# Moving two projections and a weight product in the second layer's slot order, and spreading the first layer's row sums with float32r products

## The reference, cut to what matters

```python
# layer 0, x: (16, 256, 256), 16 heads of 16
q, k = _rope(q, k)
scores = einsum('bhtd,bhsd->bhts', q, k) / sqrt(16)
probs = softmax(where(causal, scores, -inf), axis=-1)    # the division by the row sums
out = einsum('bhts,bhsd->bhtd', probs, v)                # heads side by side, (b, t, 256)
x = x + out @ w_out.T + b_out
...
# layer 1, 16 heads of 64, segments of 128 tokens
qkv = (s * rsqrt(mean(s * s) + eps) * g_norm) @ W_qkv    # q and k are rotated
...
x = x + concat_heads(attn @ v) @ W_out
```

## Time and profile before

| what | value |
|---|---|
| median of 3 runs | 2428.9 us (2425.71 to 2430.02) |
| the profiled execution's own time | 2429.98 us |
| its span, first to last instruction | 2428.1 us |
| busy over the span | PE 93%, DVE 76%, ACT 53%, POOL 42% |
| mean granted TensorE clock | 0.977 of full |
| chain that ended last, by engine | PE 57%, DVE 19%, POOL 10%, issue 8%, ACT 4% |

### The profile page before, as it was taken

The page is one execution under the profiler, slowest core; times in us unless marked ns, Lnnn a source line. Parts: engine busy times, 40 slices in busy tenths (PEclk is TensorE's granted clock), DMA queues, the critical chain, the costliest instruction groups (busy, mean ns, idle before and its releaser), DMA issues.

```text
span 2428.1 us, 53715 instructions
## 1 busy us (share of the span) xinstructions
PE 2250.7 (93%) x18240; PEld 2042.6 (84%) x18240; DVE 1853.8 (76%) x5119; ACT 1289.7 (53%) x3839; POOL 1019.6 (42%) x1078
## 2 busy tenths in 40 slices
PE   4799999999976799999999999899999999999999
PEld 3688878888865678878878878899999999999999
DVE  5878888888878667666666665578878888888876
ACT  1666666666662455555555655334336555555522
POOL 5535454454524465465465454033332222222073
PEclk8999999999987899999999999999999999999999
DMA  4523333233330322222222223221126677777443
GB/s 137 174 93 103 107 95 116 89 114 95 99 110 3 99 53 60 70 58 58 73 57 57 73 50 82 64 36 41 40 87 219 231 232 238 235 229 239 144 120 124
DMA packets 203301, 267.36 MB, mean 110 GB/s; under 512 B 61670, under 2 KB 171510, under 8 KB 192278
## 3 DMA queue, kind: packets, MB, share of 16 engines
q1 hardware_dynamic: 194166, 245.27, 33.3%
q0 software_dynamic: 8864, 18.66, 3.0%
HBM read 175.84 MB, written 43.94 MB: 91 GB/s over the span
## 4 chain that ended last, share of the span: by engine, by line
PE 57%; DVE 19%; POOL 10%; issue 8%; ACT 4%; DMA 1%; POOLq 0%; SPq 0%; DVEq 0%; ACTq 0%
PE bank L55 48%; PE bank L136 6%; POOL P L1796 3%; DVE Ph L821 2%; DVE xe L928 2%; POOL Qn L1821 1%; POOL Qn L1819 1%; DVE qm L917 1%; DVE xe L933 1%; PE bank L1322 1%; DVE sgs L955 1%; ACT Ph L657 1%; DVE rot0s L881 1%; PE bank L1362 1%; POOL Pm L1801 1%
## 5 line engine op out<-in xcount | busy, mean ns | idle before, releaser
L1495 ACT ACTIVATE P<-P,mx 128x144 f32<-128x144 f32 x512 | 206.2, 405 | 257.9 <-DVE mx L1616 256.9
L2642 POOL DMA_INDIRECT xE<-d_y,ixs x78 | 111.6, 1431 | 336.5 <-PE bank L136 306.0
L55 PE MATMUL bank<-xD_hi,w1e_lo 128*128 128x256 f32 x880 | 251.1, 285 | 0.0
L55 PE MATMUL bank<-w2e_hi,hrD_hi 128*128 128x256 f32 x880 | 249.0, 283 | 0.0
L55 PE MATMUL bank<-w2e_lo,hrD_hi 128*128 128x256 f32 x880 | 248.9, 283 | 0.0
L55 PE MATMUL bank<-w2e_hi,hrD_lo 128*128 128x256 f32 x880 | 248.9, 283 | 0.0
L55 PE MATMUL bank<-xD_lo,w1e_hi 128*128 128x256 f32 x880 | 245.9, 279 | 0.0
L55 PE MATMUL bank<-xD_hi,w1e_hi 128*128 128x256 f32 x880 | 245.6, 279 | 0.0
L1127 POOL TENSOR_TENSOR xe<-xe 128x704 f32<-128x704 f32 (+3 forms) x64 | 88.0, 1376 | 355.7 <-DVE xe L936 355.4
L1796 POOL TENSOR_TENSOR P<-P,rs 128x512 f32<-128x512 f32 x128 | 133.1, 1040 | 244.8 <-DVE rs L1625 241.2
L2251 ACT ACTIVATE hD<-bank,b1E 128x256 f32<-128x256 f32 x312 | 127.0, 473 | 197.2 <-PE bank L55 187.9
(11 more groups left out here) (324 smaller groups left out, 7871.9 us busy)
## 6 DMA issues: line engine op xcount, KB each, us to landing
w1raw<-in_ew SPq DMA_DIRECT2D x39, 1024.0 KB, 6.0
w2raw<-in_ew SPq DMA_DIRECT2D x39, 1024.0 KB, 4.8
stack<-d_rot SPq DMA_DIRECT2D x256, 96.0 KB, 2.7
K<-Kn SPq DMA_DIRECT2D x256, 72.0 KB, 2.0
d_rot<-QKh SPq DMA_DIRECT2D x64, 256.0 KB, 3.1
Q<-Qn SPq DMA_DIRECT2D x256, 64.0 KB, 2.0
d_ys<-oE SPq DMA_DIRECT2D x39, 256.0 KB, 2.6
d_rot<-QKl SPq DMA_DIRECT2D x32, 256.0 KB, 3.1
```

The lines of the kernel that those rows point to most:

```text
L55: inst = e.matmul(out, l, r, start=k == 0, stop=k == len(pairs) - 1)
L1495: inst = e.activation(P1[t % 2][:, n, :], P1[t % 2][:, n, :], ACT.Exp, bias=mx1[t % 2][:, 2 * g + sg:2 * g + sg + 1], scale=-1.0, accum_ou ...
L2642: e.indirect_dma_start(out=xE[q % 2][c], out_offset=None, in_=d_y, in_offset=bass.IndirectOffsetOnAxis(ap=ixs[r % 4][:, c:c + 1].bitcast(U ...
```

## The change

It has two parts that have nothing to do with each other. In the second layer's attention, `project(b+1, 2)` goes ahead of slot 1's `turn_heads`, `project(b+1, 3)` goes from slot 2 to the end of slot 1, and `back(b-1, 0)` goes ahead of slot 2's `turn_heads`. The waits of each step stay with it. In the first layer, DVE splits the reciprocals into a float32r part and the rest (two more DVE instructions of 32 columns, each waiting for the one before), in a zeroed 128 x 2 x 128 tile `rsp`; the transposes then give 128 rows, ACT copies 128 rows, and two float32r products on 128 rows with a 0/1 matrix that adds the two parts take the place of two float32 products on 16 rows. `sel0` grows to 128 rows, and once, at the start, ACT makes a float32r copy of it and POOL clears `rsp`.

```diff
-        w_out0, rsT, OT0 = tile("w_out0", 2, 256), tile("rsT", 256), tile("OT0", 2, 256)
+        w_out0, rsT, OT0 = tile("w_out0", 2, 256), tile("rsT", 256, dt=F32R), tile("OT0", 2, 256)
...
+        rsp, sel0r = tile("rsp", 2, 128, dt=F32R), tile("sel0r", 2, 128, dt=F32R)
...
-                turn(e, [(banks[6][0:16, st * 128:st * 128 + 128], rs0[b % 2][:, st, :]) for st in range(2)]
+                turn(e, [(banks[6][:, st * 128:st * 128 + 128], rsp[:, st, :].bitcast(F32)) for st in range(2)]
...
-                    inst = e.matmul(halves(7)[:, G, :], sel0[0:16, G, :], rsT[0:16, :], start=True, stop=True)
+                    inst = e.matmul(halves(7)[:, G, :], sel0r[:, G, :], rsT, start=True, stop=True)
...
-                e.activation(rsT[0:16, :], banks[6][0:16, 0:256], ACT.Copy).then_inc(c_rsT, 1)
+                e.activation(rsT, banks[6][:, 0:256], ACT.Copy).then_inc(c_rsT, 1)
...
+                e.activation(sel0r, sel0, ACT.Copy)
...
-                e.reciprocal(rs0[b % 2], rs0[b % 2]).then_inc(v_ri, 1)
+                if b:
+                    e.wait_ge(p_rsT, b)
+                else:
+                    e.wait_ge(g_V, 2)
+                inv, hi, lo = rs0[b % 2], rsp[:, :, 0:16], rsp[:, :, 16:32]
+                e.reciprocal(inv, inv).then_inc(*vs.up())
+                e.wait_ge(s_v, vs.n)
+                e.tensor_copy(hi, inv).then_inc(*vs.up())
+                e.wait_ge(s_v, vs.n)
+                e.tensor_tensor(lo, inv, hi.bitcast(F32), ALU.subtract).then_inc(v_ri, 1)
...
+            e.memset(rsp.bitcast(F32), 0.0)
...
+                    if s == 1:
+                        project(b + 1, 2)
                     if s == 2:
-                        project(b + 1, 3)
+                        back(b - 1, 0)
                     if s == 3:
                         squares(entering(b))
...
                     if s == 1:
-                        project(b + 1, 2)
-                    if s == 2:
-                        back(b - 1, 0)
+                        project(b + 1, 3)
```

More of the change, by code:

```diff
@@ L178, in program @@
         b_v0 = tile("b_v0", 2, 256)
-        tile("space_q", 552)
+        rsp, sel0r = tile("rsp", 2, 128, dt=F32R), tile("sel0r", 2, 128, dt=F32R)
+        tile("space_q", 40)
         qr = [tile(f"qr{i}", 44) for i in range(2)]
@@ L313, in sync_ab @@
             load_in(0)
-            for dst, src in ((raw0, "w_qkv0"), (b_qk0, "b_qk0"), (rot0, "rot0k"), (sel0[0:16], "sel0"),
+            for dst, src in ((raw0, "w_qkv0"), (b_qk0, "b_qk0"), (rot0, "rot0k"), (sel0, "sel0"),
                              (w_out0, "w_out0"), (b_out0, "b_out0")):
@@ L2744 @@
     A["w_out0"] = T2(np.ascontiguousarray(g["L0_attn_w_out"].T[rows]))
-    sel = np.zeros((16, 2, 128), np.float32)
+    sel = np.zeros((128, 2, 128), np.float32)
     for r in range(256):
-        sel[rows[r] // 16, r // 128, r % 128] = 1.0
+        sel[rows[r] // 16::16, r // 128, r % 128][0:2] = 1.0
     A["sel0"] = sel
```

## The result

The changed kernel takes 2443.8 us (median of 7 runs, 2437.0 to 2445.4), the kernel before 2430.0 in its 7 runs beside them. The ratio is 1.005, with 95% between 1.004 and 1.006: slower by half a per cent, about 14 us. The forecast was 2450 us, in a range from 2437 to 2464, so the sign and the range held and the size was about 6 us too large. The profiled execution took 2441.84 us (span 2439.9, clock 0.973), 11.9 us more than the profiled one of before.

What follows compares the result with a forecast made beforehand. The prediction took DVE's chain to bound the first layer's slots 0 and 1, PE mostly the rest. First layer +28 us (14 x 1.76 + 1 + 2), second -5.6, sum +22: 2450 us, range 2437 to 2464.

Steps and rivals of the forecast that it cites:

- The rival in which PE's 0.7 us come off whole: First layer: PE's work is the bound, so 14 x 0.7 us is saved beside the second layer's 5.6: 2413 us, chance 0.07.
- The first layer's price: First layer's DVE chain: maxima 3.45 us later, less 1.3 and 0.39 given back, net 1.76 us per batch, 14 batches.
- POOL's line 1129 gets in, and the subtraction ends at about 436.9: First layer's split: after the copy's wait, POOL's next instruction goes first and the subtraction waits it out; maxima 3.45 us later.
- the pair at 39 us: Earlier trace: DVE lines 933 and 936 each waited out a POOL instruction; taken as the nearest model for copy and subtraction.
- the rival with one POOL instruction waited out: First layer's split: only one POOL wait, maxima 1.85 us later, net 1.2 us per batch: 2441 us, chance 0.17.
- the forecast case: First layer's split: copy and subtraction each wait out a POOL instruction, 1.76 us per batch; the whole forecast's chance was 0.50.
- PE's wait at the transposes: First layer, `turn_sums`: PE waits for the subtraction, about 2.6 us idle per batch.
- The clock: First layer, slots 0 and 1: PE's waits lower the granted clock in one or two steady batches, +2 us, ends 0 and +20.
- The second layer: Second layer's attention: most of slot 1's wait moves to slot 2, 0.4 us less per batch, -5.6 us over 14 batches.
- The fourth rival: Second layer gives nothing, the delayed copies of slot 2 being the new wait: 2456 us, chance 0.12.
- The first projections of the second layer, and the last `back`, fall in stretches where PE waits for others: nothing: Second layer's start and end: moving these calls costs or saves nothing, since PE waits for others there.
- The first rival: First layer's split: one POOL instruction waited out, not two, 1.2 us per batch: 2441 us, chance 0.17.

Runs made afterwards that it cites:

- e5: The changed kernel with DVE writing only the rounded reciprocal, one instruction in place of three, low part left out: 2444.9 us, ratio 1.0010.
- e1: The changed kernel with PE's old order in the second layer, so only the first layer's part: 2443.7 us, ratio 1.0047.
- e9: The changed kernel with VectorE's rotation of projection 2 one slot earlier and the last batch's output projection in its old place: 2442.2 us, ratio 0.9987.
- e4: The changed kernel with an unused 32-column reciprocal between copy and subtraction, delaying the subtraction by 0.4 us: 2453.3 us, ratio 1.0093.
- e3: The changed kernel with the reciprocal and its split ahead of the DVE instruction that releases POOL's line 1138: 2440.5 us, ratio 1.0035.
- e2: The kernel before with only the second layer's new PE order: 2431.8 us, ratio 1.0002.
- e7: The kernel before with the second layer's new PE order, except the last batch's output projection stays in its old place: 2437.8 us, ratio 0.9979.
- e8: The kernel before with the new second-layer PE order, rotation of projection 2 a slot earlier, last batch's output projection in its old place: 2419.2 us, ratio 0.9901.

## Why the prediction was right, and where its sizes were off

**What bounds the kernel.** Right. PE's share of 96% wasn't the bound of slots 0 and 1: it did 4 us in 100 less work and the batch got longer, and e5, which keeps the saving on PE and has the old DVE chain, gives 41.80 us. The rival in which PE's 0.7 us come off whole is refuted by it.

**The first layer's price: 1.76 us per batch forecast, 1.12 measured.** This is the mis-sized term. The copy was as forecast (about 1.6 us, ending with POOL's first instruction). The step that failed is "POOL's line 1129 gets in, and the subtraction ends at about 436.9". I had transferred it from the pair at 39 us, where POOL's next instruction came ahead. Here it lost by 0.01 us, so the rival with one POOL instruction waited out came true, in its parts too: 1.85 us later forecast and 1.82 measured, with 0.39 given back at the old line 928. Only the old 917 gives back 0.37 where that rival had 0.25. This isn't a toss from batch to batch: in each of the 15 batches from the second on, in this trace and in those of e1 and e9, the subtraction starts 0.01 us before POOL's instruction. What differs from the pair at 39 us is how soon after POOL's end the waiting instruction is done: POOL's next one starts 0.08 us after the end of the one before in both places, but line 933 was done 0.15 us after that end (40.40 against 40.25) and the copy 0.04 (399.13 against 399.09). Line 917, in the earlier trace rows, was done after 0.05, which spoke for the rival. Whether the number of columns makes this difference (256 against 32 and 44) wasn't tried. e4 shows that the forecast case exists 0.4 us further on. Rows that differ by hundredths from a tie were no ground for giving the one case three times the chance of the other. From the second reciprocal to the one before the last it is 13 periods with 1.14 us each on average, 14.8 us.

The Trainium skill (SBUF — State Buffer, section Who interferes with whom) has VectorE and GpSimd excluding each other on a shared port pair, the first to start holding it to its end. The traces agree for both kinds: the copy 1.56 us behind POOL and 0.18 without it (e3), the subtraction 1.33 us behind it and 0.19 ahead of it (e4). With POOL second, its line 1140 lasts 1.73 us beside the subtraction and 1.67 without it (e4): 0.06 us more, although 0.18 us of the subtraction are left when it starts, so that row doesn't show POOL held to the subtraction's end. What the rule leaves to the trace is who arrives first.

**PE's wait at the transposes.** Forecast 2.6 us, measured 0.80, since the subtraction ends 1.6 us earlier than I had it; the rest of DVE's delay shows as 1.47 us ahead of the projection. I had written that this second wait would hide; it is the larger one.

**The clock.** Forecast +2 us for one or two steady batches. The window from 300 to 400 us has 1.00 as before, and the 12 steady periods lie between 42.89 and 43.26 us, so this term is zero there. In the second layer's last batch the clock did fall: the window from 1508 to 1518 us has 0.83, where the same wait of 1.81 us for ACT in the kernel before is followed by ten us at 1.00 (1500 to 1510). e2's trace has the same 0.83 in its window from 1490 to 1500. These are the five us that start 10 us after the last batch's first scores in e1, e7 and e8 (the granted clock is the third number from the end):

```profile
1515.53:1520.53 5.00, 4.68 (x38) 3.60 (x39) 2.20 (x17) 3.20 (x15) 2.53 (x4) 0.71 0.65 178
1494.49:1499.49 5.00, 4.83 (x38) 3.58 (x39) 2.17 (x17) 2.65 (x12) 2.52 (x4) 0.66 0.70 207
1476.07:1481.07 5.00, 4.15 (x43) 3.15 (x44) 2.19 (x17) 3.78 (x18) 2.52 (x4) 1.00 0.69 205
```

So the new order isn't needed for the fall (e1 has the old one), and e7 and e8, with the same order in this batch, differ. Of all eleven traces only those of the kernel before and of e8 have 1.00 there. What decides it stays open.

**The second layer.** Forecast -0.4 us per batch, measured -0.34, by the steps given: no wait in slot 1, 1.34 us (1.2 forecast) ahead of `back`, slot 2 6.50 instead of 6.89 us. The fourth rival, that this part gives nothing, is refuted in the periods, yet its total came true in another way: e2's ratio is 1.0002. The step that failed is "The first projections of the second layer, and the last `back`, fall in stretches where PE waits for others: nothing". I had not looked at `back(14, 0)`, in the batch whose slots have no projections. That batch costs 4.3 us more, almost what the other 14 give. e7 shows that 3.6 of it come from this one call's place (60.9 us in e2, 57.3 in e7, the clock fallen in both). The rest goes with the clock: e8 has e7's order in this batch, 1.00 where e7 has 0.66, and 56.4 us.

**Between the stages.** Forecast +1 us for batch 15, and nothing besides. The last period of the reciprocals is 2.0 us longer (52.62 against 50.59), the stretch behind it up to the second layer 2.75 us shorter, together -0.7. e1 and e9, with the same first layer, have the same pair (52.4 and 76.9, 52.7 and 76.8). PE's waits for POOL's `hq` in this stretch are 14.5 us in the changed kernel's trace and 16.9 in that of before. That the first layer ends late isn't enough to explain it: e3's last reciprocal is 10.1 us later than that of the kernel before and e4's 21.8, and their stretches are 79.7 and 78.8 us. The cause stays open.

The sum in the forecast's own terms, in the traces: the +24.6 became +14.8; the clock's +2 and batch 15's +1, with the last period, became -0.7; the -5.6 became -5.0; and three things weren't in it, -0.8 in the filling phase before the second reciprocal, +4.3 in the last batch and -0.7 at the end. 22 became 12. That the measured median lies only 6 us from the forecast is in part luck: the first layer was put some 10 us too high, and the last batch's loss was missing. The first rival, with 2441, is nearer, and its steps are the ones that the rows show.

## What to carry to other kernels

Before adding a short VectorE instruction, look at what GpSimd has in work at that moment: 32 columns cost 1.56 us here against 0.18, and the order of two instructions within hundredths of a us decides whether a second wait follows, so price both cases, and don't give one of them three times the chance of the other without a row that shows the order. When an engine's order is changed in a loop, follow it in the last iteration, where the work that covered it is missing. And when a moved instruction only moves a wait, move what it now waits for: the same reorder was worth nothing alone and 21 us with one VectorE rotation a slot earlier.

## What the runs showed of the hardware

VectorE's wait for GpSimd's instruction shows as the waiting instruction's duration, 1.56 and 1.33 us where 0.18 and 0.19 are the work, and not as idle time. The order at this place repeats to 0.01 us in 45 batches of three traces. The reciprocal of 32 columns shows no such wait: in e4 it starts at 403.48, 0.01 us before POOL's instruction, and takes 0.35 us as elsewhere, and POOL's isn't longer.

The chips differ by more than the change is worth. On the three chips of these experiments the kernel before had 2432.5, 2442.0 and 2444.9 us. The traces from different chips agree up to the end of the second layer's attention (slots of the same kernel parts within some hundredths) and part behind it. From the product with `xD` shown above to the end it is 879.7 to 883.0 us in the four traces of the first chip, 891.1 to 895.5 in the four of the second and 898.3 in e9's, and the code is the same there. A part of it is in the idle time in which PE waits for nothing that the profile shows ("issue"). Over this whole stage it is 3.4 to 6.3 us in the traces of the first chip and 10.3 to 14.8 in those of the other two. What makes a chip slower there wasn't tried.
